# Attention scores as three reduced-precision products in a fused transformer block, with the filling jobs reordered

## The chip, the cores and the metric

The kernel runs on one NeuronCore of one Trainium2 chip. The metric is the device time of one execution in microseconds (us); several executions are timed and their median is compared. Engines: PE is TensorE (matmuls, with PEld its weight loads), DVE is VectorE, ACT is ScalarE, POOL is GpSimd, SP is SyncE, which issues most transfers.

## The reference

Four sequences of 512 tokens, width 512, 16 heads of 32, all in fp32: causal attention with residual and layer norm, then a gated feed-forward block of width 2048 with residual and layer norm.

```python
qkv = jnp.einsum('bsd,ed->bse', x, w_qkv) + b_qkv
scores = jnp.einsum('bhqd,bhkd->bhqk', q, k) / math.sqrt(Hd) + causal
attn = softmax(scores)
x = _layernorm(x + einsum(attn @ v, w_out) + b_out)
g, u = x @ Wg.T, x @ Wu.T            # weights: (integers - 128) * scale
x = _layernorm(x + (silu(g) * u) @ Wd.T)
```

## The kernel before

**Groups and steps.** The work of attention is 16 groups, G = 0 to 15: batch `b`, `g` = G % 4, four heads each (HG), whose queries or keys fill 128 partitions. Each group is run in 16 steps (STEPS) by every engine's program in the same written order: the order is fixed by hand tables, not by a scheduler, and each engine is an in-order queue.

**What a group holds.** `scores(G, qbs)` makes the scores of a 128-query tile for four heads, one product per head on its 32 rows of the array, in full fp32: `q_sb` by `k_sb`, widths 128, 256, 384, 512 by the causal mask. Tile 2 (384 wide) comes at step 0, tile 3 (512) at step 3, and tiles 0 and 1 (128 and 256) of the next group at step 8. VectorE's `tile_max` (L1131) scales, masks and takes the negative maximum; ScalarE's `exponential` (L922) follows. Ten transpose tasks (TASK_STEPS 0, 0, 3, 8, 8, 10, 10, 12, 12, 15, L1469), four 128x128 transposes each, turn the probabilities; even tasks are evicted by ScalarE (L978), odd ones by VectorE (L509). `weighted_values` (L1490) multiplies them with the values at step 8 and at the next group's step 0. `normalise`, `att_hi` and `att_lo` (L749, POOL) scale the result and split it into a high and a low fp32r part.

**Filling jobs.** Between these, TensorE works off `filling(G)`: a list of jobs of 12 products of 512 columns each (MM) and a count of products for each step. A job is the queries or the keys of the group two ahead (`project`, L1391), a value tile (`project_values`, L1409) or an output tile (`project_out`, L1427), all in three fp32r products: high by high, low by high, high by low. ENDED holds the step after that in which a job's last product stands; there the job is evicted by VectorE: `queries_or_keys` (L1117) adds the bias and writes fp32, `values` (L1122), `outputs` (L1182, with layer norm's statistics).

**Banks.** Transposes and jobs share three PSUM banks, assigned ahead by class `Banks`: the bank that was freed longest ago is next. TensorE waits (`work_drained`) until the eviction of the bank's last user is done. Four banks hold the scores, one (`pv_acc`) the weighted values.

**Other queues.** ScalarE scans the feed-forward weights for their largest value (`scan`, L942) twice in most groups, after steps 6 and 14, when a 1 MB transfer (`load_scan`) has landed; in the third group of a batch it makes the high half of the next batch's x (`next_hi`, L912, `xT_hi`), after POOL's `join`, which waits until the batch's last keys are done; POOL makes the low half (`next_lo`). SP issues transposing transfers (`turn`, `load_short`), and for w_out `turn_w`, in place of `w_stage`'s value tiles.

**Start.** Weight tiles are transposed on TensorE and split by `w_hi` (ACT) and `w_lo` (DVE) in the order of `transpose_weights`; `project` of the first batch waits for its tile's low half.

Of the kernel before, what the change touches and what calls it, by code (L numbers as in the profile page):

```python
# [6 lines left out]
def postln_block_kernel(nc: bass.Bass, x, w_qkv, b_qkv, w_out, b_out, gate_w, gate_scale, up_w, up_scale,  # L7
# [78 lines left out]
    SLOTS = 7  # L86
    X_STEPS = [1, 2, 3, 4]
    X_FIRST = [3, 4, 5, 6]
# [27 lines left out]

    def filling(G):
        b, g = divmod(G, NG)
        ahead = [("q", G + 2), ("k", G + 2)] if G + 2 < GROUPS else []
        if G == 0:  # L120
            return [("v", 0, t) for t in range(NT)], EVEN
        if G == 1:
            return [("q", 2), ("k", 2), ("q", 3)], [8, 0, 0, 4, 0, 4, 8, 0, 3, 0, 3, 0, 3, 0, 0, 3]
        if G == 2:
            return [("k", 3)] + ahead, [8, 4, 0, 0, 0, 0, 0, 0, 6, 0, 6, 0, 6, 0, 0, 6]
        if g == 0:
            return [("v", b, QH), ("v", b, QH + 1)] + ahead, EVEN
        if g == 1:
            return [("o", b - 1, 0), ("o", b - 1, 1)] + ahead, EVEN
        if g == 3:  # L130
            return ([("v", b + 1, 0), ("v", b + 1, 1)] + ahead, EVEN) if b < LAST else ([], [0] * STEPS)
        before = [("o", b - 1, t) for t in range(QH, NT)]
        return (before + ahead, AMONG_X) if b < LAST else (before, AMONG_X[:8] + [0] * (STEPS - 8))
# [7 lines left out]
    def x_at(G, s):  # L141
        return [c for c in range(ND) if (X_STEPS if G > NG else X_FIRST)[c] == s] if G % NG == 2 else []
# [17 lines left out]

    class Banks:

        def __init__(self):
            self.uses, self.ended, self.busy, self.now = [0] * (WORK + HG), list(range(-WORK - HG, 0)), {}, 0
# [18 lines left out]
        def part(self, jobs, done, count):  # L183
            for n in range(done, done + count):
# [7 lines left out]
                ("w", 3), ("q", 1), ("w", 4), ("w", 5), ("k", 1), ("w", 6), ("w", 7))  # L192
# [78 lines left out]
    with ctx:  # L271
# [34 lines left out]
        attT_hi, attT_lo, v_tok = [None] * 2, [None] * 2, [None] * 2  # L306
        attT_hi[1] = sb("attT_hi1", [P, NG, S], F32R, att)
        attT_lo[1] = sb("attT_lo1", [P, NG, S], F32R, att)
        v_tok[1] = sb("v_tok1", [P, NT, D], F32, att)
        scan_buf = sb("scan_buf", [P, NT, D], F32, att)  # L310
        attT_hi[0] = sb("attT_hi0", [P, NG, S], F32R, att)
        attT_lo[0] = sb("attT_lo0", [P, NG, S], F32R, att)
        v_tok[0] = sb("v_tok0", [P, NT, D], F32, att)
        q_sb = [sb(f"q_sb{i}", [P, S], F32, att) for i in range(2)]
        k_sb = [sb(f"k_sb{i}", [P, S], F32, att) for i in range(2)]
# [67 lines left out]
        score, work, pv_acc = bank[0:HG], bank[HG:HG + WORK] + bank[0:HG], bank[HG + WORK]  # L383
# [1356 lines left out]
```

## Time and profile before

| what | value |
|---|---|
| median of 3 runs | 728.05 us (726.4 to 728.89) |
| the profiled execution | 730.08 us |
| its span | 728.3 us |
| PE busy | 705.8 us (97%), 4296 matmul records |
| DVE, ACT, POOL busy | 385.6, 366.3, 187.7 us |
| granted TensorE clock | 0.996 of full speed |
| attention | about the first 347 us; then feed-forward |

A record of an fp32 product appears twice in the trace (two records a product); a reduced-precision product has one. A record's duration includes its way through the array, so the next one's start tells what a product costs. In the chain of waits each step is followed back to what released it; the timeline merges equal neighbours (xN).

### The profile page before, as it was taken

How to read it: one execution, taken by the hardware profiler on the slowest of the kernel's cores; microseconds unless marked ns; L12 is line 12 of the kernel's file. 1: busy time of each engine (PE TensorE's matmuls, PEld its weight loads, DVE VectorE, ACT ScalarE, POOL GpSimd, SP SyncE). 2: the span in 40 equal slices, each digit the busy share in tenths (PEclk: the TensorE clock that was granted, in tenths of full speed). 3: DMA queues.
4: the chain of work that ended last, by engine and by line, in shares of the span. 5: the costliest groups of instructions: out<-in, count | busy, mean ns of one | idle time of the engine just before them, and what ended most of it. 6: DMA issues, size and time to landing. Idle time of an engine off the chain costs nothing.

```text
span 728.3 us, 11598 instructions
## 1 busy us (share of the span) xinstructions
PE 705.8 (97%) x4296; PEld 546.0 (75%) x4296; DVE 385.6 (53%) x999; ACT 366.3 (50%) x886; POOL 187.7 (26%) x192
## 2 busy tenths in 40 slices
PE   7999899999999999999999999999999999999994
PEld 6777577677777777676687888888888888888883
DVE  3767566666667766578452223553344533544335
ACT  3766677677676766578655654222232222322230
POOL 0000633446131661219753242220010002000004
PEclk9999999999999999999999999999999999999998
DMA  9753675526774376704788944951430013000111
GB/s 306 178 140 102 154 95 189 130 75 135 171 231 96 98 146 207 216 22 125 181 154 206 198 138 144 228 187 43 145 102 13 0 43 130 1 0 1 59 58 60
DMA packets 106246, 89.33 MB, mean 123 GB/s; under 512 B 70352, under 2 KB 80592, under 8 KB 106064
## 3 DMA queue, kind: packets, MB, share of 16 engines
q1 hardware_dynamic: 99664, 68.69, 34.5%
q0 software_dynamic: 6528, 19.93, 12.4%
q8 instruction: 33, 0.54, 0.3%
q14 instruction: 21, 0.17, 0.1%
HBM read 63.20 MB, written 23.30 MB: 119 GB/s over the span
## 4 chain that ended last, share of the span: by engine, by line
PE 81%; SPq 8%; DMA 4%; POOL 2%; DVE 2%; ACT 1%; issue 1%; POOLq 0%; DVEq 0%
PE bank L1604 15%; PE bank L1605 15%; PE bank L1391 11%; PE bank L1469 8%; PE bank L1612 7%; PE bank L1611 7%; PE bank L1452 5%; PE bank L1409 5%; PE bank L1427 4%; PE bank L1490 4%; SPq L564 2%; DMA scan_buf<-in_L_ffn_up_w_dram 2%; SPq L623 1%; SPq L620 1%; SPq L626 1%; DVE probs L1131 1%
## 5 line engine op out<-in xcount | busy, mean ns | idle before, releaser
L922 ACT ACTIVATE probs<-probs,neg_max 128x128 f32<-128x128 f32 (+3 forms) x256 | 140.4, 552 | 3.3 <-DVE neg_max L1131 3.1
L1131 DVE CUSTOM_DVE_ANT_0 probs<-bank,causal 128x128 f32<-128x128 f32 (+3 forms) x256 | 110.9, 485 | 42.0 <-PE bank L1452 42.0
L1264 DVE SCALAR_TENSOR_TENSOR hid<-bank,u_scale,silu 128x512 f32<-128x512 f32 x64 | 48.0, 751 | 160.2 <-PE bank L1605 153.6
L1604 PE MATMUL bank<-xT_hi,gateT 128*128 128x512 f32 x256 | 99.9, 390 | 1.2 <-DVE hid L1264 1.2
L1605 PE MATMUL bank<-xT_lo,gateT 128*128 128x512 f32 x256 | 99.8, 390 | 0.0
L1605 PE MATMUL bank<-xT_lo,upT 128*128 128x512 f32 x256 | 99.8, 390 | 0.0
L1604 PE MATMUL bank<-xT_hi,upT 128*128 128x512 f32 x256 | 99.7, 389 | 0.0
L1469 PEld LDWEIGHTS bank<-ident,probs 128*128 128x128 f32 x640 | 71.4, 140 | 36.9 <-issue 24.1
L1030 ACT ACTIVATE silu<-bank,g_scale 128x512 f32<-128x512 f32 x64 | 44.0, 687 | 102.2 <-PE bank L1605 102.2
L1469 PE MATMUL bank<-ident,probs 128*128 128x128 f32 x640 | 88.2, 277 | 4.3 <-DVE probsT L509 1.6
L978 ACT ACTIVATE probsT<-bank 128x512 f32<-128x512 f32 x80 | 47.6, 595 | 88.4 <-PE bank L1469 86.8
L1036 ACT ACTIVATE hid_hi<-hid 128x512 fp32r<-128x512 f32 x58 | 36.7, 632 | 107.1 <-DVE hid L1264 107.1
L1612 PE MATMUL bank<-downT,hid_lo 128*128 128x512 f32 x232 | 90.4, 390 | 0.0
L1611 PE MATMUL bank<-downT,hid_hi 128*128 128x512 f32 x232 | 90.3, 389 | 0.0
L509 DVE COPY probsT<-bank 128x512 f32<-128x512 f32 x80 | 54.9, 687 | 29.2 <-PE bank L1469 29.1
L749 POOL TENSOR_TENSOR attT_lo<-attT,attT_hi 128x512 fp32r<-128x512 f32 x16 | 20.7, 1294 | 166.7 <-ACT attT_hi L934 166.7
L1268 DVE TENSOR_TENSOR hid_lo<-hid,hid_hi 128x512 fp32r<-128x512 f32 x58 | 40.2, 693 | 40.5 <-ACT hid_hi L1036 40.5
L1604 PEld LDWEIGHTS bank<-xT_hi,gateT 128*128 128x128 f32 x256 | 48.1, 188 | 11.9 <-DVE hid L1264 2.0
L1391 PE MATMUL bank<-xT_hi,wT_hi 128*128 128x512 f32 x128 | 55.6, 443 | 0.6 <-POOL xT_lo L775 0.5
L1605 PEld LDWEIGHTS bank<-xT_lo,upT 128*128 128x128 f32 x256 | 48.1, 188 | 9.9
L1605 PEld LDWEIGHTS bank<-xT_lo,gateT 128*128 128x128 f32 x256 | 48.1, 188 | 9.9
L1604 PEld LDWEIGHTS bank<-xT_hi,upT 128*128 128x128 f32 x256 | 48.1, 188 | 9.9
(111 smaller groups left out, 1164.4 us busy)
## 6 DMA issues: line engine op xcount, KB each, us to landing
halves<-x_tok SPq DMA_DIRECT2D x7, 1024.0 KB, 7.4
x_tok<-halves SPq DMA_DIRECT2D x7, 1024.0 KB, 7.9
scan_buf<-in_L_ffn_gate_w_dram SPq DMA_DIRECT2D x4, 1024.0 KB, 8.2
scan_buf<-in_L_ffn_up_w_dram SPq DMA_DIRECT2D x4, 1024.0 KB, 7.7
scan_buf<-in_L_ffn_down_w_dram SPq DMA_DIRECT2D x4, 1024.0 KB, 5.1
w_int<-in_L_ffn_gate_w_dram POOLq DMA_DIRECT2D x16, 256.0 KB, 3.4
w_int<-in_L_ffn_up_w_dram POOLq DMA_DIRECT2D x16, 256.0 KB, 3.4
w_int<-in_L_ffn_down_w_dram POOLq DMA_DIRECT2D x16, 256.0 KB, 3.6
```

The lines of the kernel that those rows point to most:

```text
L509: copy(probsT[:, (G * BLOCKS + i) % SLOTS, :], bank_of("t", G, i)[:, :]).then_inc(drained_of("t", G, i), 1)
L922: nc.scalar.activation(probs[qb][:, j, :], probs[qb][:, j, :], ACT.Exp, bias=neg_max[:, qb, j:j + 1], scale=-1.0, accum_out=row_sum[:, qb, ...
L978: evict_task(act, G, i, lambda o, i: nc.scalar.activation(o, i, ACT.Copy))
L1030: nc.scalar.activation(silu[:, i % 2, :], bank[:, :], ACT.Silu, scale=g_scale[:, i:i + 1]).then_inc(silu_done, 1)
L1131: nc.vector.tensor_tensor_reduce(out=probs[qb][:, j, :], in0=score[j][:, first:first + w], in1=causal[:, S - w:S], scale=-SCALE, scalar=-F ...
L1264: nc.vector.scalar_tensor_tensor(out=hid[:, i % 2, :], in0=bank[:, :], scalar=u_scale[:, i:i + 1], in1=silu[:, i % 2, :], op0=ALU.mult, op ...
L1391: last = nc.tensor.matmul(acc[:, :], w[:, c, e], xT[:, c, :], start=at == 0, stop=at == MM - 1)
L1469: last = nc.tensor.transpose(acc[:, m * P:(m + 1) * P], probs[qb][:, j, kb * P:(kb + 1) * P], ident[:, :])
L1604: nc.tensor.matmul(acc[n][:, :], w[:, c, cols], form(xT_hi[:, c, :]), start=c == 0, stop=False)
L1605: last = nc.tensor.matmul(acc[n][:, :], w[:, c, cols], form(xT_lo[:, c, :]), start=False, stop=c == ND - 1)
L1611: nc.tensor.matmul(down_acc[t][:, :], form(hi[:, tok]), w_down[:, i, :], start=i == 0, stop=False)
L1612: return nc.tensor.matmul(down_acc[t][:, :], form(lo[:, tok]), w_down[:, i, :], start=False, stop=i == NI - 1)
```

## The change

Scores become three fp32r products: the queries and keys are stored as a high part (`q_hi`, `k_hi`) and the rest (`q_lo`, `k_lo`). The high part is written from the bank by a new ScalarE instruction with the bias, `queries_or_keys_hi`; VectorE's then writes bank + bias - high, in place of bank + bias. The filling jobs are put in another order, so that between a group's queries and keys there is a value or output tile; the keys of G3 move from G2 to G1, with other counts. In G2 the conversions of the next x stand at steps 1 to 4 instead of 3 to 6. The attention tiles are kept in a ring of six groups in place of two sets of four. w_out's transposing transfers get a place of their own (`w_turn`). At the start the second queries go ahead of the first scores, in an eighth, spare bank (that of `pv_acc`). The variance of layer norm moves from step 9 to 11 where there are keys and queries to come.

```diff
     def filling(G):
         b, g = divmod(G, NG)
-        ahead = [("q", G + 2), ("k", G + 2)] if G + 2 < GROUPS else []
+        q, k = ([("q", G + 2)], [("k", G + 2)]) if G + 2 < GROUPS else ([], [])
...
         if G == 1:
-            return [("q", 2), ("k", 2), ("q", 3)], [8, 0, 0, 4, 0, 4, 8, 0, 3, 0, 3, 0, 3, 0, 0, 3]
+            return [("q", 2), ("k", 2), ("q", 3), ("k", 3)], [8, 0, 0, 8, 0, 8, 4, 0, 14, 0, 2, 0, 2, 0, 0, 2]
         if G == 2:
-            return [("k", 3)] + ahead, [8, 4, 0, 0, 0, 0, 0, 0, 6, 0, 6, 0, 6, 0, 0, 6]
+            return q + k, [0, 0, 0, 0, 0, 2, 4, 0, 12, 0, 2, 0, 2, 0, 0, 2]
         if g == 0:
-            return [("v", b, QH), ("v", b, QH + 1)] + ahead, EVEN
+            return [("v", b, QH)] + q + [("v", b, QH + 1)] + k, EVEN
         if g == 1:
-            return [("o", b - 1, 0), ("o", b - 1, 1)] + ahead, EVEN
+            return [("o", b - 1, 0)] + q + [("o", b - 1, 1)] + k, EVEN
...
     banks.whole(("x", 0, 0), ("w", 0), ("x", 0, 1), ("x", 0, 2), ("x", 0, 3), ("w", 1), ("q", 0), ("k", 0), ("w", 2),
-                ("w", 3), ("q", 1), ("w", 4), ("w", 5), ("k", 1), ("w", 6), ("w", 7))
+                ("w", 3))
+    banks.start(("q", 1), [SPARE_BANK])
+    banks.end(("q", 1))
+    banks.whole(("w", 4), ("w", 5), ("k", 1), ("w", 6), ("w", 7))
...
+            def queries_or_keys_hi(kind, G):
+
+                wait_full(act, kind, G)
+                if G == 0:
+                    act.wait_ge(bias_qk_loaded, 16)
+                chunk = "qk".index(kind) * NG + G % NG
+                nc.scalar.activation((q_hi, k_hi)["qk".index(kind)][G % 2][:, :], bank_of(kind, G)[:, :], ACT.Identity,
+                                     bias=bias_qk[:, chunk:chunk + 1]).then_inc(qk_hi_done, 1)
...
             for G in range(GROUPS):
                 b, g = divmod(G, NG)
                 for s in range(STEPS):
+                    for job in ENDED.get(G * STEPS + s, []):
+                        if job[0] in "qk":
+                            queries_or_keys_hi(*job)
...
             def queries_or_keys(kind, G):
 
-                wait_full(dve, kind, G)
+                dve.wait_ge(qk_hi_done, 2 * G + "qk".index(kind) + 1)
                 chunk = "qk".index(kind) * NG + G % NG
-                nc.vector.tensor_scalar((q_sb, k_sb)["qk".index(kind)][G % 2][:, :], bank_of(kind, G)[:, :],
-                                        bias_qk[:, chunk:chunk + 1], None, ALU.add).then_inc(drained_of(kind, G), 1)
+                hi, lo = ((q_hi, q_lo), (k_hi, k_lo))["qk".index(kind)]
+                nc.vector.scalar_tensor_tensor(out=lo[G % 2][:, :], in0=bank_of(kind, G)[:, :],
+                                               scalar=bias_qk[:, chunk:chunk + 1], in1=hi[G % 2][:, :].bitcast(F32),
+                                               op0=ALU.add, op1=ALU.subtract).then_inc(drained_of(kind, G), 1)
...
-                    if g == 2 and s == 9 and b > 0:
+                    if g == 2 and s == (11 if b < LAST else 9) and b > 0:
...
-                    for j in range(HG):
-                        rows = slice(j * HD, (j + 1) * HD)
-                        last = nc.tensor.matmul(score[j][:, first:first + w], q_sb[G % 2][rows, qb * P:(qb + 1) * P],
-                                                k_sb[G % 2][rows, 0:w], start=True, stop=True)
-                        if qb == qbs[-1]:
-                            last.then_inc(score_full[j], 1)
+                    for n, (qs, ks) in enumerate(((q_hi, k_hi), (q_lo, k_hi), (q_hi, k_lo))):
+                        for j in range(HG):
+                            rows = slice(j * HD, (j + 1) * HD)
+                            last = nc.tensor.matmul(score[j][:, first:first + w], qs[G % 2][rows, qb * P:(qb + 1) * P],
+                                                    ks[G % 2][rows, 0:w], start=n == 0, stop=n == 2)
+                            if qb == qbs[-1] and n == 2:
+                                last.then_inc(score_full[j], 1)
...
+            queries = project("q", 1)
+            for _ in range(MM // 2):
+                next(queries)
             scores(0, (0, 1))
-            for n, kind in enumerate("qk"):
-                for _ in project(kind, 1):
-                    pass
-                transpose_weights(2 * n + 4)
-                transpose_weights(2 * n + 5)
+            for _ in queries:
+                pass
```

**How the order moves.** ScalarE in G5 around step 7; `scan_buf` is the scan, `probsT` an evicted transpose task, `probs` an exponential. Before, and then after:

```order
L922 ACTIVATE probs,row_sum<-probs,neg_max 128x512 [waits max_done] x4
L942 ACTIVATE scan_buf,scan_sums<-scan_buf,minus_exact 128x1024 [waits scan_loaded]
L978 ACTIVATE probsT<-bank 128x512 [waits work_full0]
L922 ACTIVATE probs,row_sum<-probs,neg_max 128x128 [waits max_done] x4
L978 ACTIVATE probsT<-bank 128x512 [waits work_full0]
```
```order
L940 ACTIVATE probs,row_sum<-probs,neg_max 128x512 [waits max_done] x4
L968 ACTIVATE scan_buf,scan_sums<-scan_buf,minus_exact 128x1024 [waits scan_loaded]
L959 ACTIVATE q_hi<-bank,bias_qk 128x512 [waits work_full0]
L1012 ACTIVATE probsT<-bank 128x512 [waits work_full2]
L940 ACTIVATE probs,row_sum<-probs,neg_max 128x128 [waits max_done] x4
L1012 ACTIVATE probsT<-bank 128x512 [waits work_full2]
```

The high half of the queries stands behind the scan and ahead of task 4's eviction.

VectorE in G4 at the same steps (`v_tok` a value tile, the ISA rows 128 wide the maxima of the next group, COPY the eviction of task 3). Before, and then after:

```order
L1122 TENSOR_TENSOR v_tok<-bank,bias_v 128x512 [waits work_full0]
L1131 ISA probs,neg_max<-bank,causal 128x128 [waits score_full0]
L1131 ISA neg_max 128x1
L1131 ISA probs,neg_max<-bank,causal 128x128 [waits score_full1]
L1131 ISA neg_max 128x1
L1131 ISA probs,neg_max<-bank,causal 128x128 [waits score_full2]
L1131 ISA neg_max 128x1
L1131 ISA probs,neg_max<-bank,causal 128x128 [waits score_full3]
L1131 ISA neg_max 128x1
L509 COPY probsT<-bank 128x512 [waits work_full1]
```
```order
L1152 SCALAR_TENSOR_TENSOR q_lo<-bank,bias_qk,q_hi 128x512 [waits qk_hi_done]
L1167 ISA probs,neg_max<-bank,causal 128x128 [waits score_full0]
L1167 ISA neg_max 128x1
L1167 ISA probs,neg_max<-bank,causal 128x128 [waits score_full1]
L1167 ISA neg_max 128x1
L1167 ISA probs,neg_max<-bank,causal 128x128 [waits score_full2]
L1167 ISA neg_max 128x1
L1167 ISA probs,neg_max<-bank,causal 128x128 [waits score_full3]
L1167 ISA neg_max 128x1
L531 COPY probsT<-bank 128x512 [waits work_full0]
```

Where the second value tile was taken, the low half of the queries is, and it waits for ScalarE's.

TensorE at the start, from the fourth weight tile (`w_stage`) on. Before, and then after:

```order
L1357 MATMUL bank<-ident,w_stage 128x128 [waits work_drained0,w_loaded3]
L1357 MATMUL bank<-ident,w_stage 128x128 x3
L1452 MATMUL bank<-k_sb,q_sb 128x128 [waits work_drained1,work_drained0]
L1452 MATMUL bank<-k_sb,q_sb 128x128 x3
L1452 MATMUL bank<-k_sb,q_sb 128x256 x4
L1391 MATMUL bank<-xT_hi,wT_hi 128x512 [waits work_drained1,work_drained2]
L1391 MATMUL bank<-xT_hi,wT_lo 128x512
```
```order
L1393 MATMUL bank<-ident,w_stage 128x128 [waits work_drained0,w_loaded3]
L1393 MATMUL bank<-ident,w_stage 128x128 x3
L1427 MATMUL bank<-xT_hi,wT_hi 128x512 [waits work_drained2]
L1427 MATMUL bank<-xT_hi,wT_lo 128x512
L1427 MATMUL bank<-xT_lo,wT_hi 128x512
L1427 MATMUL bank<-xT_hi,wT_hi 128x512
L1427 MATMUL bank<-xT_hi,wT_lo 128x512
L1427 MATMUL bank<-xT_lo,wT_hi 128x512
L1489 MATMUL bank<-k_hi,q_hi 128x128 [waits work_drained1,work_drained0]
L1489 MATMUL bank<-k_hi,q_hi 128x128 x3
L1489 MATMUL bank<-k_hi,q_lo 128x128 x4
L1489 MATMUL bank<-k_lo,q_hi 128x128 x4
```

Half of the second queries' product now stands ahead of the first scores, and with it the wait for the third weight tile's low half.

## Rows read from the trace of the kernel before

**Rows 1.** Busy time by stretch, G1, G2, G3, G12: length, then each engine's busy us
```profile
47.44:67.64 20.20, 19.59 (x168) 13.87 (x172) 14.49 (x46) 13.17 (x40) 1.99 (x2) 1.00 0.44 96
...
67.64:90.10 22.46, 19.66 (x160) 13.13 (x164) 13.41 (x45) 14.39 (x42) 11.12 (x10) 1.00 0.63 158
...
90.10:111.46 21.36, 21.36 (x172) 15.44 (x176) 13.83 (x45) 14.58 (x42) 6.31 (x6) 1.00 0.74 101
...
283.95:306.84 22.89, 21.58 (x173) 15.42 (x169) 13.82 (x45) 14.46 (x42) 6.92 (x6) 1.00 0.76 233
```

**Rows 2.** Chain of waits in G3 and G14: start us, us, what (x records)
```profile
95.47 1.07 PE bank L1452 x8
...
103.47 1.40 PE bank L1391 x6
...
104.87 0.87 PE bank L1469 x8
...
328.28 0.86 PE bank L1452 x8
```

**Rows 3.** Timeline of TensorE in G3: start us, us, engine, line, operation
```profile
91.68 0.93 PE L1452 MATMUL bank<-k_sb,q_sb 32*128 32x384 f32 x8
...
101.51 0.94 PE L1452 MATMUL bank<-k_sb,q_sb 32*128 32x128 f32 x16
...
102.38 1.09 PE L1469 MATMUL bank<-ident,probs 128*128 128x128 f32 x8
...
104.70 1.04 PE L1469 MATMUL bank<-ident,probs 128*128 128x128 f32 x8
...
106.96 1.04 PE L1469 MATMUL bank<-ident,probs 128*128 128x128 f32 x8
```

**Rows 4.** Timeline of ScalarE and VectorE in G3
```profile
100.16 0.71 ACT L922 ACTIVATE probs<-probs,neg_max 128x512 f32<-128x512 f32 x1
...
100.86 1.14 ACT L942 ACTIVATE scan_buf<-scan_buf,minus_exact 128x1024 f32<-128x1024 uint32 x1
...
102.47 0.29 DVE L1131 CUSTOM_DVE_ANT_0 probs<-bank,causal 128x128 f32<-128x128 f32 x1 [0.94 <-PE bank L1452]
...
103.31 0.69 DVE L509 COPY probsT<-bank 128x512 f32<-128x512 f32 x1
...
105.72 0.69 DVE L509 COPY probsT<-bank 128x512 f32<-128x512 f32 x1
```

**Rows 5.** Groups of instructions by line and shape: busy us, mean ns, idle before
```profile
L1264 DVE SCALAR_TENSOR_TENSOR hid<-bank,u_scale,silu 128x512 f32<-128x512 f32 x64 | 48.0, 751 | 160.2 <-PE bank L1605 153.6 <-ACT silu L1030 6.6
...
L978 ACT ACTIVATE probsT<-bank 128x512 f32<-128x512 f32 x80 | 47.6, 595 | 88.4 <-PE bank L1469 86.8
```

**Rows 6.** Timeline at the start: keys' eviction, third tile, scores, second queries
```profile
17.00 0.75 DVE L1117 TENSOR_SCALAR k_sb<-bank,bias_qk 128x512 f32<-128x512 f32 x1 [1.90 <-PE bank L1391]
...
18.06 1.29 DVE L1103 TENSOR_TENSOR wT_lo<-bank,wT_hi 128x512 fp32r<-128x512 f32 x2 [0.31 <-ACT wT_hi L898]
...
18.81 0.51 PE L1391 MATMUL bank<-xT_hi,wT_hi 128*128 128x512 f32 x1
...
21.71 1.04 PE L1357 MATMUL bank<-ident,w_stage 128*128 128x128 f32 x8
```

**Rows 7.** Timeline of ScalarE: first scan of G4, G6, G8, G12
```profile
122.89 1.13 ACT L942 ACTIVATE scan_buf<-scan_buf,minus_exact 128x1024 f32<-128x1024 uint32 x1
...
166.10 1.14 ACT L942 ACTIVATE scan_buf<-scan_buf,minus_exact 128x1024 f32<-128x1024 uint32 x1
...
209.00 1.15 ACT L942 ACTIVATE scan_buf<-scan_buf,minus_exact 128x1024 f32<-128x1024 uint32 x1 [1.24 <-DMA scan_buf<-in_L_ffn_gate_w_dram]
...
297.11 1.15 ACT L942 ACTIVATE scan_buf<-scan_buf,minus_exact 128x1024 f32<-128x1024 uint32 x1 [3.88 <-DMA scan_buf<-in_L_ffn_up_w_dram]
```

**Rows 8.** Timeline of TensorE in G2: the wait before transpose task 4
```profile
80.38 0.66 PE L1469 MATMUL bank<-ident,probs 128*128 128x128 f32 x4 [1.17 <-ACT probs L922]
```

**Rows 9.** Chain of waits where the feed-forward part begins
```profile
382.99 3.97 DMA stage<-down_short
```

More of the change, by code:

```diff
@@ L141, in x_at @@
     def x_at(G, s):
-        return [c for c in range(ND) if (X_STEPS if G > NG else X_FIRST)[c] == s] if G % NG == 2 else []
+        return [c for c in range(ND) if X_STEPS[c] == s] if G % NG == 2 else []
     FILLING = [filling(G) for G in range(GROUPS)]
@@ L159, in postln_block_kernel @@
     OUT_STEP, EARLY, LATE = 2, (QH, QH + 1), (0, 1)
+    SPARE_BANK = WORK + HG
     class Banks:
         def __init__(self):
-            self.uses, self.ended, self.busy, self.now = [0] * (WORK + HG), list(range(-WORK - HG, 0)), {}, 0
+            self.uses, self.ended, self.busy, self.now = [0] * (SPARE_BANK + 1), list(range(-SPARE_BANK - 1, 0)), {}, 0
             self.count = WORK
@@ L382, in postln_block_kernel @@
         bank = [ctx.enter_context(nc.psum_tensor(f"bank{i}", [P, 512], F32)) for i in range(8)]
-        score, work, pv_acc = bank[0:HG], bank[HG:HG + WORK] + bank[0:HG], bank[HG + WORK]
+        score, work, pv_acc = bank[0:HG], bank[HG:HG + WORK] + bank[0:HG] + bank[HG + WORK:], bank[HG + WORK]
         gate_acc, up_acc, down_acc = bank[0:4:2], bank[1:4:2], bank[4:8]
@@ L408, in postln_block_kernel @@
         res_ready = sem("res_ready")
-        work_full = [sem(f"work_full{i}") for i in range(WORK + HG)]
-        work_drained = [sem(f"work_drained{i}") for i in range(WORK + HG)]
+        work_full = [sem(f"work_full{i}") for i in range(SPARE_BANK + 1)]
+        work_drained = [sem(f"work_drained{i}") for i in range(SPARE_BANK + 1)]
         x_hi_done = sem("x_hi_done")
+        qk_hi_done = sem("qk_hi_done")
         score_full = [sem(f"score_full{j}") for j in range(HG)]
@@ L574, in turn_w @@
             def turn_w():
-                for t in range(NT):
-                    wait_full(sp, "w", w_tile("v", t))
                 for e in range(2 * ND):
@@ L949, in _ @@
             x_hi(3)
-            for i in range(1, 4):
-                w_hi(i)
+            w_hi(1)
+            queries_or_keys_hi("q", 0)
+            queries_or_keys_hi("k", 0)
+            w_hi(2)
+            w_hi(3)
             for j in range(HG):
                 exponential(0, 0, j)
+            queries_or_keys_hi("q", 1)
             w_hi(4)
@@ L1426, in project_out @@
                     for n, (a, w) in enumerate(((att_hi, wT_hi), (att_hi, wT_lo), (att_lo, wT_hi))):
-                        last = nc.tensor.matmul(acc[:, :], a[:, c, tok], w[:, c, NE:NE + D], start=c == 0 and n == 0,
+                        last = nc.tensor.matmul(acc[:, :], a[:, tok], w[:, c, NE:NE + D], start=c == 0 and n == 0,
                                                 stop=c == NG - 1 and n == 2)
@@ L1478, in weighted_values @@
                     pe.wait_ge(normed, G)
+                if m == 0 and G == 0:
+                    wait_drained(pe, "q", 1)
                 hf, kb, _, qbs = TASKS[PRODUCTS[m][0]]
@@ L1516, in _ @@
             transpose_weights(3)
+            queries = project("q", 1)
+            for _ in range(MM // 2):
+                next(queries)
             scores(0, (0, 1))
[L1518 to L1522 removed]
+            for _ in queries:
+                pass
+            transpose_weights(4)
+            transpose_weights(5)
+            for _ in project("k", 1):
+                pass
+            transpose_weights(6)
+            transpose_weights(7)
             outs = [project_out(B - 1, t) for t in range(NT)]
```

47 lines of the change are left out of this document (28 added, 19 removed).

## The prediction, made before the changed kernel was run

> **What bounds it now.** I read four views, in this order: the page, the busy time by stretch, TensorE's timeline of one group, and the other engines' timeline of the same stretch. G0 to G15 are the sixteen groups in the kernel's order; a group is counted here from its 384-wide scores. The page puts TensorE at nearly all of the span. G3, like most groups, lasts 21.36 us with TensorE busy for all of it, while VectorE has 13.8 and ScalarE 14.6 us of work [rows 1]: in attention what counts is TensorE's own work, plus any wait that comes to stand in it. G1 and G2 are the exceptions, 20.20 and 22.46 us with 0.6 and 2.8 us of idle TensorE [rows 1] (the stretches there begin 1.6 us sooner, with the values' products); they have 36 projection products each instead of 48.
>
> **Scores, removed and added.** Per group and tile the full-precision score costs, up to the next work: 0.86 us (384 wide), 1.07 (512) [rows 2] and 0.87 (128 and 256 together, 101.51 to 102.38 [rows 3]), 2.80 in all. Eight records of 512 columns in 1.07 us can only be four heads side by side. 512 less 384 columns is 0.21 us more, that is 1.64 ns a column or four passes of 0.41 ns; 1280 columns make 2.10 to 2.15 us, and 0.65 to 0.70 us is switching, which stays. The change makes three passes of the same columns, with weights loaded anew for each. Two bounds for a pass: 0.41 ns a column, as above, gives 1.60 us for all and a gain of 0.53; or no pass is shorter than one 128-column load with its product, which the eight probability transposes show as 0.87/8 = 0.109 us, and a wide one costs what the reduced-precision projection costs, 1.40/6 = 0.233 us for 512 [rows 2]: 128 and 256 then take 3 x 0.11 each, 384 takes 3 x 0.17, 512 takes 3 x 0.22 to 0.233, 1.8 to 1.95 in all and a gain of 0.2 to 0.35. I take 0.33, since the loads are in the kernel: **-5.3 us** over 16 groups (-3 to -8.5).
>
> **Evicting queries and keys.** VectorE's tensor_scalar took 0.75 us from the bank [rows 6] and its successor is a scalar_tensor_tensor, 751 ns in the feed-forward part [rows 5]: nothing. New is ScalarE's copy of the high half, 0.60 us like its evictions of transposes [rows 5], 32 times. ScalarE has 14.6 busy of 21.4 us, so its sum is no bound. Its place in the queue is. In the new order the queries end with the 24th product, at step 7, where before the second value or output tile ended. On ScalarE their copy stands behind the first scan of the group; on VectorE the low half stands before the four 128-wide maxima and the eviction of transpose task 3. Task 5 and the second value tile reuse banks that these free. In G3, times from its start at 91.68: the scan starts at 9.18 and takes 1.14 [rows 4]; then high half 0.60, hand-over 0.05, low half 0.75, maxima 0.84 (102.47 to 103.31), copy of task 3 0.69, hand-over 0.05. Task 3's bank is free at scan start + 4.12, less 0.28 since the 384 and 512 scores came sooner. TensorE wants it at 13.02 (104.70 [rows 3]) less the 0.34 that the three scores save. The wait is scan start - 8.84. Before, the maxima started at 10.79 and the bank was free a microsecond before it was wanted.
> Scan starts in G3, G5, G7, G9, G11, G13 are 9.18 (one pattern; G3's row stands for six): 0.34 each, 2.0 us. G4 9.85 (122.89 [rows 7]): 1.0. G6 and G10, where ScalarE also converts the next batch's x, 10.35 (166.10): 1.5 each, 3.0. G8 10.52, late because its data came late (209.00): 1.7. G12 13.16 (297.11), data 3.9 us late: 4.3, of which the kernel already pays 1.5 (that group lasts 22.89 where others last 21.36 [rows 1]): 2.8. That is 10.5 us. VectorE then has as much left before task 5's copy as before, 2.41 us from one copy's start to the next's (103.31 to 105.72 [rows 4]), where TensorE needs 2.26 (104.70 to 106.96): 0.15 more in 11 groups, 1.65. Together **+12.2 us** (5 to 15). What is queued behind: ScalarE's exponentials 128 wide, which wait for the maxima and have slack until the group's end. The keys' copy comes at the group's end, with 3.2 us of other TensorE work (values product, 384 scores, two transpose tasks) before its bank is wanted and 1.35 of eviction: nothing, and if the second scan is late, 0.3.
>
> **G1 and G2.** The fourth keys move to G1: 12 products more there, 2.8 us, less the 0.6 it waited: +2.2. In G2 they go, and the join of the next x can start at G1's end. But nothing now stands between its 384 and 512 scores. G2 becomes 15.8 us of work (21.36 less 24 products of 0.233) and waits: 1.25 for the four maxima, 0.75 for the pieces of x, 0.95 for task 2's eviction, 0.7 for the exponentials, as ScalarE does four conversions and an extra copy there. 19.45 against 22.46 is -3.0, with +2.2: **-0.8 us** net (+0.5 to -2.5; today's G2 waits 1.17 us for the exponentials at the same task [rows 8]).
>
> **Start.** The keys' bank is full at 17.00 [rows 6]. Now ScalarE makes the high half before the third weight tile's, VectorE the low half (to 18.40) before that tile's (to 19.05), and the second queries' product, which needs the tile, goes ahead of the scores: it starts at 19.1 with TensorE idle from 17.7. Six products 1.45, scores 0.91 (17.90 to 18.81), six more 1.45: 22.9 where today it is 21.71 [rows 6]. The same chain once more (keys of group 1, two weight tiles, values wait for the last of them) adds 0.4 in G0: **+1.6 us** (0.5 to 2.5).
>
> **The rest.** The feed-forward part starts behind SyncE's row of transposing loads that begins with G14's join and ends with a load that lands at 386.96 [rows 9]; what G14 and G15 save is waited for there: **+0.6**. The ring of six for the attention tiles, the extra bank and w_turn need no new wait that comes late: the output tiles of a batch are done at the end of its successor's third group, the first of these slots is rewritten in the fourth. The variance moved to step 11 follows its last output tile, and its readers are the next group's. 128 more instructions' issue lies beside running products.
>
> **Sum**: -5.3 +12.2 -0.8 +1.6 +0.6 = +8.3 us. The profiled execution took 730.08 us (span 728.3), 2.0 above the median 728.05 of the runs; against the median: **736.4 us**. About 0.3%, 2.2 us, is what a measurement of this kernel can tell from none.
>
> **Rivals.** (a) *The hand-over hides.* The largest term hangs on a queue place that I shift by sums. Were ScalarE at the queries' copy 1 us sooner than reckoned, only G6, G8, G10 and G12 would wait, 3.5 us in all: 736.4 - 8.7 = 727.7. With 2 us, only G12, 0.8: 725.0; with 1 us and passes at column rate 724.5. The sign turns at waits of 12.2 - 8.3 = 3.9 us. For it: today's steady groups show no TensorE wait at all, and both engines are a third idle. Against it: the last exponential and the scan follow each other without a gap (100.16, 100.86 [rows 4]). (b) *It comes out even*: passes at column rate (-8.5), waits of 9 us, the rest as above: +1.9 us, 730.0. (c) *The heads don't run side by side* in reduced precision, so twelve passes stand in a row: 1280 columns x 12 x 0.41 ns = 6.3 us in place of 2.1 a group, +67 us, 803. Against it: nothing in the rows but the lack of such a product; the four heads of full precision start within one record. (d) *More waits than reckoned*, by the late data of G8 and G12 growing: waits 18 us, 742.2. That the edit leaves the scores as they were is excluded: TensorE's order has the 12 products.
>
> **Chances.** My forecast 0.48, (d) 0.12, (b) 0.13, (a) 0.25, (c) 0.02. Faster by over 0.3%: 0.25, within: 0.13, slower: 0.62. The forecast's own range is 731 to 741.5; with (a), (b) and (d), and the bounds of scores and waits, 722.5 to 744.
>
> **What would show it.** Score tiles: 512 to the next work about 0.9 us, 384 about 0.74, 128 and 256 about 0.85; 0.75, 0.70 and 0.70 would mean column rate. In G3 and G5 TensorE idle 0.3 to 0.5 us before the second value tile or task 5, released by VectorE's low half of q or its copy; in G6 and G10 1.5 to 1.8; in G12 over 4. G2 about 19, G1 about 22. If ScalarE's q copies come before 10.0 us of a group and TensorE's groups last 21.0, (a) is right and I am wrong.

## The result, and the profile after

The changed kernel took 737.72 us (median of 4 runs, 737.05 to 739.69) beside 727.22 us (725.83 to 728.89) for the kernel before in the same comparison: ratio 1.0117, interval 1.0074 to 1.0159. Slower, as predicted, and 1.3 us from the 736.4. The difference that was forecast is 8.3 us; between these medians it is 10.5, and in a later comparison (735.55 us beside 729.13, ratio 1.008, 1.0055 to 1.0105) it is 6.4. The profiled spans are 735.4 and 728.3 us, 7.1 apart. Of the experiments' executions, one of 1164.12 us among the twelve of pool_queries and one of 736.35 us, the profiled one, among the ten of both are left out of the ratios below as slow, but not out of the medians.

The page of the changed kernel, first the span, then TensorE's busy time (x instructions):

```profile
span 735.4 us, 12142 instructions
...
PE 704.1 (96%) x4552; PEld 551.8 (75%) x4552; DVE 386.2 (53%) x999; ACT 386.7 (53%) x918; POOL 188.2 (26%) x192
```

TensorE is busy 1.7 us less than before in a span 7.1 us longer: the loss is idle TensorE. Busy time by stretch for G1, G2, G3, G4, G6 and G12 (length; then PE, PEld, DVE, ACT, POOL; clock, DMA), as in [rows 1]:

```profile
48.97:72.32 23.35, 22.33 (x196) 16.62 (x192) 15.36 (x47) 15.82 (x44) 3.42 (x4) 1.00 0.39 97
72.32:92.40 20.08, 16.52 (x165) 11.24 (x162) 12.61 (x43) 15.44 (x44) 9.82 (x9) 1.00 0.44 122
92.40:113.67 21.27, 21.26 (x188) 15.86 (x184) 13.73 (x45) 15.86 (x44) 6.32 (x6) 1.00 0.88 152
113.67:135.65 21.98, 21.31 (x190) 15.87 (x186) 13.73 (x45) 17.82 (x48) 11.94 (x10) 1.00 0.52 151
157.11:180.53 23.42, 21.80 (x188) 15.75 (x185) 15.56 (x50) 17.71 (x48) 13.93 (x12) 1.00 0.35 86
289.97:312.70 22.73, 21.29 (x189) 15.87 (x185) 13.73 (x45) 15.96 (x44) 6.93 (x6) 1.00 0.77 225
```

G3 is hardly shorter (21.27 for 21.36), G4 is 0.6 us longer, G6 2.1. The scores themselves did what the sum said. The chain of waits in G3: scores 384 wide, 512 wide, 128 and 256 wide:

```profile
92.47 0.73 PE bank L1489 x12
...
96.07 0.90 PE bank L1489 x10
...
102.00 0.89 PE bank L1489 x21
```

0.73 + 0.90 + 0.89 = 2.52 us where it was 2.80 [rows 2, 3]: 0.28 saved. Behind them the first wait shows in TensorE's timeline of G3:

```profile
102.81 1.09 PE L1506 MATMUL bank<-ident,probs 128*128 128x128 f32 x8
103.92 0.50 PE L1445 MATMUL bank<-wT_hi,xT_hi 128*128 128x512 f32 x1
```

From these transposes (tasks 3 and 4) to the next work it is 1.11 us, where the trace of before has 0.85 (102.38 to 103.23). In G4, G6 and G12 waits are plain to see. TensorE's timeline of these (the bracket is the idle time before, and what ended it; L1445 is a value product, L1427 a projection):

```profile
125.87 0.50 PE L1445 MATMUL bank<-wT_hi,xT_hi 128*128 128x512 f32 x1 [0.67 <-DVE q_lo L1152]
...
165.75 0.50 PE L1427 MATMUL bank<-xT_hi,wT_hi 128*128 128x512 f32 x1 [1.19 <-POOL xT_lo L793]
...
166.99 0.50 PE L1427 MATMUL bank<-xT_hi,wT_hi 128*128 128x512 f32 x1 [0.28 <-POOL xT_lo L793]
...
302.94 0.50 PE L1445 MATMUL bank<-wT_hi,xT_hi 128*128 128x512 f32 x1 [1.45 <-DVE q_lo L1152]
```

G4 and G12 stop for the low half of the queries, as forecast. G6 stops for something that my sum did not have: the next batch's x. ScalarE and VectorE in G4, the hand-over itself:

```profile
123.23 1.13 ACT L968 ACTIVATE scan_buf<-scan_buf,minus_exact 128x1024 f32<-128x1024 uint32 x1
...
124.36 0.67 ACT L959 ACTIVATE q_hi<-bank,bias_qk 128x512 fp32r<-128x512 f32 x1
...
125.06 0.75 DVE L1152 SCALAR_TENSOR_TENSOR q_lo<-bank,bias_qk,q_hi 128x512 fp32r<-128x512 f32 x1 [3.36 <-ACT q_hi L959]
```

And GpSimd in G6, which begins at 157.11: the join, then the low halves, of which the last two end at 166.9, 9.8 us into the group. In the old order the queries' products, which read them, began at step 8, 11.5 us into the group (167.29 less 155.75 in the trace of before); now they begin at step 5, 5.9 us into it.

```profile
155.67 4.46 POOL L788 COPY x_whole<-x_tok 128x1024 uint16<-128x1024 uint16 x4 [13.24 <-PE bank L1427]
160.09 2.65 POOL L793 TENSOR_TENSOR xT_lo<-x_whole,xT_hi 128x512 fp32r<-128x512 f32 x2
...
164.42 2.52 POOL L793 TENSOR_TENSOR xT_lo<-x_whole,xT_hi 128x512 fp32r<-128x512 f32 x2
```

Where the feed-forward part begins, the chain waits 4.70 us for the landing that took 3.97 in [rows 9], and TensorE's stop behind it is 2.64 us, where the trace of before has 1.19:

```profile
389.38 4.70 DMA stage<-down_short
...
394.10 1.33 ACT downT L1034 x2
```

### The profile page after: what moved, and what is told of

It reads as the page before. It is cut to its first block, busy times and chain, and to the rows that moved or that the text cites. A ratio compares the mean times of both kernels' runs of the same rounds, so it can differ in the third digit from the quotient of the medians.

```text
span 735.4 us, 12142 instructions
## 1 busy us (share of the span) xinstructions
PE 704.1 (96%) x4552; PEld 551.8 (75%) x4552; DVE 386.2 (53%) x999; ACT 386.7 (53%) x918; POOL 188.2 (26%) x192
## 4 chain that ended last, share of the span: by engine, by line
PE 77%; ACT 6%; SPq 5%; DMA 4%; DVE 4%; POOL 2%; issue 1%; POOLq 0%; DVEq 0%
PE bank L1649 15%; PE bank L1650 15%; PE bank L1506 8%; PE bank L1427 8%; PE bank L1657 7%; PE bank L1656 7%; PE bank L1445 5%; PE bank L1529 4%; PE bank L1489 4%; PE bank L1463 4%; ACT probs L940 3%; DMA scan_buf<-in_L_ffn_up_w_dram 2%; DMA scan_buf<-in_L_ffn_gate_w_dram 2%; SPq L639 2%; SPq L642 1%; SPq L645 1%
## 5 line engine op out<-in xcount | busy, mean ns | idle before, releaser
L1506 PEld LDWEIGHTS bank<-ident,probs 128*128 128x128 f32 x640 | 69.5, 140 | 28.2 <-DVE probsT L531 12.2
L1649 PEld LDWEIGHTS bank<-xT_hi,gateT 128*128 128x128 f32 x256 | 48.1, 188 | 13.3 <-DVE hid L1300 3.4
L1427 PE MATMUL bank<-xT_hi,wT_hi 128*128 128x512 f32 x128 | 52.9, 421 | 4.7 <-POOL xT_lo L793 3.2
L768 POOL TENSOR_TENSOR attT_lo_front<-attT,attT_hi_front 128x512 fp32r<-128x512 f32 x12 | 15.5, 1291 | 137.4 <-ACT attT_hi_front L951 137.4
```

The costliest lines, as they stand in the source:

```text
L1427: last = nc.tensor.matmul(acc[:, :], w[:, c, e], xT[:, c, :], start=at == 0, stop=at == MM - 1)
L1506: last = nc.tensor.transpose(acc[:, m * P:(m + 1) * P], probs[qb][:, j, kb * P:(kb + 1) * P], ident[:, :])
L1649: nc.tensor.matmul(acc[n][:, :], w[:, c, cols], form(xT_hi[:, c, :]), start=c == 0, stop=False)
```

## The experiments

One table first, since the runs are read by the lengths of groups (us, between the starts of the 384-wide scores in each trace) and by the ratio to the kernel before. The first four experiments ran on one chip, the next seven on another, the last on a third.

| kernel | G1+G2 | G3 | G4 | G6 | G8 | G12 | median us | ratio (95%) |
|---|---|---|---|---|---|---|---|---|
| before | 42.66 | 21.36 | 21.36 | 21.36 | 21.36 | 22.89 | | |
| changed | 43.43 | 21.27 | 21.98 | 23.42 | 21.97 | 22.73 | 737.72 | 1.0117 (1.0074-1.0159) |
| copy_first | 43.44 | 21.04 | 21.04 | 23.41 | 21.05 | 21.03 | 732.79 | 1.004 (1.0004-1.0076) |
| outputs_first | 43.44 | 21.28 | 21.98 | 21.80 | 22.64 | 22.44 | 735.11 | 1.0104 (1.0055-1.0152) |
| scores_alone | 45.32 | 21.81 | 21.80 | 21.81 | 21.81 | 21.83 | 736.24 | 1.0107 (1.0059-1.0156) |
| order_alone | 41.91 | 21.30 | 21.32 | 23.52 | 21.30 | 21.30 | 730.17 | 1.0017 (0.9996-1.0037) |
| both | 43.44 | 21.02 | 21.05 | 21.82 | 27.10 | 21.03 | 731.31 | 1.0017 (0.9986-1.0048) |
| copies_alone | 43.82 | 21.32 | 21.31 | 22.07 | 23.27 | 21.83 | 733.29 | 1.004 (1.0008-1.0072) |
| pool_queries | 42.36 | 21.07 | 21.09 | 21.09 | 24.92 | 21.09 | 730.00 | 0.9995 (0.9971-1.0018) |
| changed, again | 44.90 | 21.30 | 22.00 | 23.42 | 21.88 | 22.05 | 735.55 | 1.008 (1.0055-1.0105) |
| pool_late_scan | 42.36 | 21.10 | 21.10 | 21.07 | 21.08 | 21.07 | 727.22 | 0.9963 (0.9933-0.9993) |
| before_late_scan | 42.60 | 21.35 | 21.36 | 21.38 | 21.36 | 21.36 | 729.06 | 0.9978 (0.9948-1.0008) |
| pool_late_old_start | 42.36 | 21.08 | 21.10 | 21.11 | 21.09 | 21.09 | 726.43 | 0.9956 (0.9931-0.9982) |
| scales_by_pool | 42.39 | 21.08 | 21.10 | 21.09 | 21.07 | 21.10 | 731.58 | 1.0022 (0.9992-1.0052) |

**copy_first.** The changed kernel, the first scan one step later, so behind the queries' copy on ScalarE.

```diff
-    ... for G in SCAN_GROUPS[1:] for s in (6, 14)]
+    ... for G in SCAN_GROUPS[1:] for s in (7, 14)]
```

> The changed kernel with the first scan of a group one step later, so that on ScalarE the queries' high half stands ahead of it. Theory A (the hand-over behind the scan is what costs): groups 4 and 8 fall from 21.97 us to about 21.1, G12 from 22.73 to 21.3, the plain ones from 21.28 to 21.05, and G6 and G10 from 23.43 to 21.1; in all 9 to 10 us less than the changed kernel, about 728. Theory B (in G6 and G10 the queries' product waits for the next x's low half, now that it stands three steps sooner, and the copy is not to blame there): those two stay above 22.8, the others fall as in A; 5 to 6 us less, about 732. Theory C (the loss is in the first three groups and at the end): under 1.5 us less.

Measured 732.79 us, as B had it. Busy time by stretch of G4 and G6 in this run:

```profile
114.33:135.37 21.04, 21.04 (x189) 15.96 (x186) 13.73 (x45) 17.60 (x48) 11.94 (x10) 1.00 0.54 160
156.54:179.95 23.41, 21.82 (x189) 15.75 (x185) 15.65 (x50) 17.82 (x48) 13.91 (x12) 1.00 0.35 84
```

G4 has no idle TensorE left, G3 lost 0.23, G12 1.70; so these waits were the copy's place behind the scan. G6 did not move: there the copy was never what TensorE waited for. 21.04 us is what a full group takes with the new scores.

**outputs_first.** The changed kernel, with the third groups' jobs in the old order.

```diff
-        return [("o", b - 1, QH)] + q + [("o", b - 1, QH + 1)] + k, (
+        return [("o", b - 1, QH), ("o", b - 1, QH + 1)] + q + k, (
```

> The changed kernel with the old job order in the third groups alone: both output tiles, then queries, then keys. Theory A: the queries' copy no longer stands behind the scan at step 7 in G6 and G10, their whole excess of 2.1 us over a plain group goes, 4 us less. Theory B: TensorE's stops before products that read the next x's low half (1.8 us in G6, as much in G10) go, 3.6 to 4.8 us less; the stop named there in the trace is POOL's xT_lo in the changed kernel and none here. The two agree on the sum; what tells them apart is the length of G6 in the run with the copy first. Theory C: nothing to speak of.

G6 fell by 1.6 us to 21.80, less than either theory had: the stop for xT_lo is gone, but another has come, 0.69 us before the keys' first product, released by VectorE's low half of the queries; scores_alone explains it. G8 gave 0.7 us back, its scan's data having landed later. The ratio cannot be told from the changed kernel's 1.0117; it is the trace that decides here.

**order_alone.** The kernel before with the new job order, counts and variance step; scores in full precision, one eviction.

> The kernel before (full-precision scores, one VectorE eviction) with the new job order, the new counts of G1 and G2, the earlier conversions in G2 and the later variance. Theory A: no ScalarE copy, no hand-over, so G3 to G13 stay at 21.36 and G6, G10 too; only G1 and G2 change, within 1 us: ratio 1.000. Theory B: G6 and G10 are 1.8 us longer each, plus 0.8 for G1 and G2 together: +4.4 us, 1.006.

B: G6 is 23.52 us and the stop is the same, without any copy. TensorE's timeline of this run in G6:

```profile
162.03 0.50 PE L1391 MATMUL bank<-xT_hi,wT_hi 128*128 128x512 f32 x1 [1.00 <-POOL xT_lo L775]
...
163.28 0.50 PE L1391 MATMUL bank<-xT_hi,wT_hi 128*128 128x512 f32 x1 [0.28 <-POOL xT_lo L775]
```

So the late x costs 2.2 us in each of G6 and G10 (21.36 to 23.52), 4.3 in all. G1 and G2 gain 0.75 us by their new counts. The whole, 1.0017, is not the 1.006 that B expected: it cannot be told from before. In this trace G12, whose data came sooner, is 1.6 us shorter than before, and G0 begins 1.7 us sooner.

**scores_alone.** The changed kernel with the old jobs, counts, banks and start.

> The changed kernel with the jobs, the counts, the banks and the start of the kernel before: the three-product scores and the two-part evictions alone. If the scores save what the changed kernel's groups show (0.28 us) and the copies hide, 16 groups give 4.5 us less than before, ratio 0.994, groups of 21.07 us. If the copies still stop TensorE in each group (0.25), ratio 0.999. If the old order with keys at once behind queries makes the copies stand in each other's way (what the reordering would be for), 1.005 or more.

The third case. Every group from G3 on is 21.81 us, 0.77 over the full 21.04. TensorE's timeline in G6 of this run, the keys' first product:

```profile
154.68 0.51 PE L1424 MATMUL bank<-xT_hi,wT_hi 128*128 128x512 f32 x1 [0.69 <-DVE q_lo L1149]
```

In the old order the queries end at step 10 and the keys want the bank two transpose tasks (1.0 us, 152.95 to 153.95) later, while copy and low half, one after the other, hold it for 1.5 us (153.15 to 154.62), though both engines stood idle before them. In a plain group the copy costs more here than in the new order (0.77 us against 0.27), which pays for this with the late x; in the whole time the two orders cannot be told apart (1.0107 and 1.0117).

**both.** The two edits together.

> The changed kernel with both edits: queries' high half ahead of the scan, and output tiles first in the third groups. If the two causes add up fully, G6 and G10 fall from 23.4 us to 21.1 and the time is 4.5 us below the run with the copy first alone, ratio to before 0.998. If, as the run with the scores alone suggests (21.81 us in every group), queries that end at step 10 with the keys at once behind them stop TensorE by 0.7 us, G6 and G10 come to 21.8: 3.2 us below the copy first alone, ratio 1.000.

The second case: G6 is 21.82 (the same 0.69 us stop), and the two edits give 731.31 us, no different from before. The profiled execution (736.35 us) lost 6 us in G8, where the scan's data came 14.8 us into the group.

**copies_alone.** As both, with one full-precision product a score, of the high halves:

```diff
-                    for n, (qs, ks) in enumerate(((q_hi, k_hi), (q_lo, k_hi), (q_hi, k_lo))):
...
+                        last = nc.tensor.matmul(score[j][:, first:first + w],
+                                                q_hi[G % 2][rows, qb * P:(qb + 1) * P].bitcast(F32),
+                                                k_hi[G % 2][rows, 0:w].bitcast(F32), start=True, stop=True)
```

> The same as the run with both edits, but each score is again one full-precision product, of the high halves read as fp32 (8 records in place of 12 a tile); the low halves are made and not read, so the scores leave out the low parts. What the three products save is then read directly: 0.28 us a group by the traces so far, 4.5 us in all (my prediction took 5.3; the column rate would be 8.5): this kernel should be 1.006 times the one with both edits, with groups of 21.3 us where that has 21.04.

Groups without a wait: 21.32 against 21.02, as expected; 0.28 to 0.3 us is what the scores save. The medians differ by 2.0 us, with intervals that overlap: the trace decides here, not the times.

**pool_queries.** The chain of two evictions on one bank is taken away. VectorE alone empties the bank, as before; GpSimd makes both halves later, from SBUF. The jobs of G3 on stand in the old order.

```diff
+        return G > 1 and (kind == "q" or G == 2)
...
+                if by_pool(kind, G):
+                    nc.vector.tensor_scalar(qk_full[:, :], bank_of(kind, G)[:, :],
+                                            bias_qk[:, chunk:chunk + 1], None, ALU.add).then_inc(drained_of(kind, G), 1)
...
+                nc.gpsimd.tensor_copy(hi, full).then_inc(split_hi, 1)
+                nc.gpsimd.tensor_tensor(lo, full, hi.bitcast(F32), ALU.subtract).then_inc(split_done, 1)
```

> The changed kernel with the old job order in groups 3 to 15 (first groups' new counts kept). The queries (and the keys of G2) are evicted by VectorE alone, bank plus bias in fp32, as before the change, and GpSimd makes their high and low halves from that copy later; the keys are copied as in the change. If the chain of two evictions on one bank is what costs (A), TensorE never waits in a plain group: 21.04 us, G1 and G2 together 41.4 us, about 5 to 6 us below the kernel before, ratio 0.993. Rival: GpSimd's 2.6 us a group beside VectorE's work make VectorE's instructions longer or come too late for the next scores: groups of 21.3 us or more, ratio 1.000.

A, in every group from G3 on but one. G1 and G2 together took 42.36 us where A had 41.4: there the rival is right in part, since in G1 TensorE stops 0.78 us before the next scores, released by GpSimd's low half of the keys. The ratio is 0.9995 and not the 0.993 of A. Busy time by stretch of G3, G6 and G8:

```profile
90.98:112.05 21.07, 21.07 (x188) 15.99 (x184) 13.82 (x45) 15.28 (x43) 8.22 (x8) 1.00 0.86 165
154.26:175.35 21.09, 21.09 (x188) 15.99 (x184) 15.47 (x50) 17.14 (x47) 14.71 (x12) 1.00 0.39 92
196.45:221.37 24.92, 22.70 (x189) 17.29 (x186) 13.92 (x45) 15.16 (x43) 8.68 (x8) 0.93 0.68 211
```

Neither VectorE's time (13.8 us) nor GpSimd's 2 us more cost anything. But G8 lost 3.8 us to a scan whose data came late, and ScalarE stood before it. ScalarE's timeline in G8:

```profile
210.25 1.15 ACT L994 ACTIVATE scan_buf<-scan_buf,minus_exact 128x1024 f32<-128x1024 uint32 x1 [4.82 <-DMA scan_buf<-in_L_ffn_gate_w_dram]
```

**The last comparison** has the changed kernel again, pool_queries with the first scan of G4, G8 and G12 at step 12 in place of 6, the kernel before with that alone, and the combination with the old start:

```diff
-    ... for G in SCAN_GROUPS[1:] for s in (6, 14)]
+    ... for G in SCAN_GROUPS[1:] for s in (6 if G % NG else 12, 14)]
```

> The changed kernel itself, on the same chip as the three others of this call, so that they have one reference: 1.010 to 1.013 times the kernel before. Its groups should repeat (21.28 plain, 21.97 for G4, 23.43 for G6 and G10), apart from G8 and G12, whose length goes by when the first scan's data land.

> The run with GpSimd splitting the queries, and the first scan of every batch's first group (G4, G8, G12) at step 12 in place of 6, since in its trace G8 lasted 24.92 us with the data landing 13.8 us into the group, and 27.1 in the run with both edits. If that wait is an in-order ScalarE standing before its data, G8 and G12 come to 21.1 whatever the landing, and the time to some 5 us below the kernel before: ratio 0.992. If the transfers themselves (their traffic) hold the group up, nothing changes: 0.9995.

> The kernel before with the first scans of G4, G8 and G12 at step 12 alone. In the trace of before G12 is 1.5 us longer than its neighbours and the data of G8 and G12 land late; if the later scan takes that away, 1.5 to 3 us less, ratio 0.997, and what remains between this kernel and the one with GpSimd is the scores' share, 4 us. If its groups are bound elsewhere: 1.000.

> The same as the run with the late scans and GpSimd's split, with the start of the kernel before (first scores ahead of the second queries, no spare bank). My prediction gave the new start +1.6 us over the old one without copies; with copies in both, this kernel should be 0.5 to 1 us slower if the new start helps to hide the copies, and equal within 0.3 us if the start is bound by the weight tiles alone. In the traces the time from the last x tile's first transpose to G0's 384-wide scores is to be compared (17.6 to 18.4 us with the new start, 18.1 with the old one).

The late scan does what the first case says: G8 is 21.08 us with TensorE busy throughout, although the data landed 14.8 us after their issue and 13.3 us into the group (13.6 and 13.9 in the two other kernels with GpSimd's split and the late scan), as late as in pool_queries (13.8). So it was the engine that stood before its data, and not the traffic. With it the kernel is faster than before, 727.22 and with the old start 726.43 us, ratios 0.9963 and 0.9956, 1.2% below the changed kernel on the same chip. I had expected 0.992. The kernel before gains by it too (0.9978, its interval includes 1), and G12 falls from 22.89 to 21.36. How much of the 0.4% is the three-product scores' and how much the late scan's is not shown: the intervals of 0.9956 and 0.9978 overlap. The changed kernel repeated 1.008, less than the 1.010 to 1.013 I had written. G1 and G2 were 1.5 us longer in it than in the first trace (44.90), to which the last section comes. The start can be read from the transposes of the third and fourth weight tiles, TensorE's last work before the two starts part, to G0's 384-wide scores. TensorE's timelines, of before and then of the changed kernel:

```profile
16.80 1.03 PE L1357 MATMUL bank<-ident,w_stage 128*128 128x128 f32 x8
...
26.62 0.93 PE L1452 MATMUL bank<-k_sb,q_sb 32*128 32x384 f32 x8
```
```profile
15.38 1.03 PE L1393 MATMUL bank<-ident,w_stage 128*128 128x128 f32 x8
...
26.26 0.45 PE L1489 MATMUL bank<-k_hi,q_hi 32*128 32x384 f32 x4
```

It is 9.76 to 9.82 us in the three kernels without copies, 11.18 to 11.24 with copies and the old start, 10.88 to 10.93 in the eight with copies and the new one. So the new start saves 0.3 us there, and half of it is lost in G0 (22.68 against 22.55 here): they are equal within 0.3 us, the second case of that expectation.

**scales_by_pool.** pool_late_old_start, with the three loads of the feed-forward scales issued by GpSimd instead of SyncE.

> The run with GpSimd's split, late scans and the old start, with the three loads of the feed-forward scales issued by GpSimd in place of SyncE. In the traces TensorE stops at the fifth tile of the feed-forward part for 1.58 us before the change and 2.9 to 3.3 us in every kernel with the three-product scores and GpSimd's split, and SyncE's row of transposing loads, which holds that tile's weights back, has 6.5 to 7 us of these three issues in it. If the row is what the saved time of the last groups is waited for (my term 'the rest'), the stop goes and the time falls by 3 us: ratio to the kernel before about 0.992. If the stop stays, it is released by something else.

The time did not fall: 731.58 us. The stop at the fifth tile (2.92 us in pool_late_old_start) is gone, but a new one of 7.03 us stands at the first down product, behind which TensorE comes to the fifth tile 8 us later (393.70 against 385.73), so that the missing stop tells nothing of SyncE's row. Nor did the row end sooner: its last load for that tile was issued 44.1 us after the start of G15, where pool_late_old_start has 41.7. The chain of waits of this run:

```profile
361.65 1.15 POOL u_scale L902
362.80 12.62 DMA d_scale<-in_L_ffn_down_scale_dram
```

## Why the prediction was right, and where it was not

The time and the sign were right; of the five terms that gave them the scores, the start and the counts of G1 and G2 were close, and the largest, the waits, was not. By the profiled executions (728.3 to 735.4 us):

- **Scores**, -5.3: 0.28 us a group, -4.5 over 16 (copies_alone has 0.30). The bound that I took from a load fits, though no run shows that it is the load: passes of 128 and 256 columns both follow each other by 0.11 us (102.09, 102.20, 102.31 and 102.48, 102.60 in TensorE's timeline of G3), those of 512 by 0.23. At column rate a pass of 128 columns would take 0.05; that rate, and with it the gain of 8.5 us, is not there. The Trainium skill ("TensorE: Matmul & The Clock Gate", section "Weight-path perf modes — Fast Weight Load (FWL) and DoubleRow") lets loads of 128 columns other than FP32 go faster; by that the narrow passes would be shorter, and the traces do not agree for these products on 32 rows. Mis-sized by 0.05: the narrow tiles gained nothing (0.87 to 0.89).
- **Hand-over behind the scan**, +12.2: mechanism and formula hold outside G6 and G10, its inputs did not. Measured against copy_first: about 0.27 in each of six groups, 0.94 and 0.92 in G4 and G8, 1.70 in G12, nothing in G6 and G10, 5.2 us in all; less the 1.5 that G12 paid before, 3.7 over the kernel before. "Scan start - 8.84" with the scan starts of this trace (those of G8 and G12 came 0.7 and 2.6 us sooner than in the trace of before, with 0.28 allowed for the scores) gives 0.31, 1.0, 1.0 and 1.75. I had taken the landings of one trace for fixed. The 0.15 for task 5 was wrong: where it shows (G5, G9, G13) order_alone has it without a copy.
- **G6 and G10**: I put 3.0 us on them for the copy, and they lost 4.1 over before, for another reason. I followed the queries' eviction into two queues and did not ask what their product reads. GpSimd's low halves could have been read from the trace of before; in the one after they end 166.9 - 157.1 = 9.8 us into the group.
- **G1 and G2**, -0.8: the counts gave -0.75 (order_alone). But the copies cost 2.1 us there (43.43 plus 0.56 for the scores, against 41.91), which I counted only from G3 on; in the trace TensorE stops 0.82 us in G1 and 0.84 in G2 before transposes, released by VectorE's eviction of a transposed tile (in G1 the queries' low half and four maxima stand ahead of it), and order_alone has neither stop. copy_first has the same 43.44, so it is not the scan.
- **Start**, +1.6: right. G0's scores began 0.36 us sooner than before only because this execution was 1.42 us ahead where the starts part (15.38 against 16.80, the transposes of the third and fourth weight tiles; the point lies between 14.58 and 16.80 in the traces, with either start). From there to G0 it is 10.88 us against 9.82, +1.06, and G0 lasts 0.31 longer though its scores save 0.28: +1.65 in all. The second queries' product starts 2.32 us behind that point (17.70), where I had 2.3 (19.1 less 16.80), with the 1.3 us stop before it.
- **The rest**, +0.6: +1.45, the stop of 1.19 us became 2.64. That it ends with SyncE's row the chains of waits show, before and after. But the row did not merely stay: from the start of G14 to the landing it is 59.9 us where it was 58.8, of which 0.7 is the last landing. scales_by_pool does not settle it, and in the other kernels with copies the stop is 1.45 to 2.92 us; why stays open.

So 8.5 us of the waits that I summed did not come, and 6.4 us that I had not summed did (2.1 in G1 and G2, 4.3 for the late x), with 0.8 more at each of scores and rest, 0.4 for task 5, and 1.4 less by the early beginning; 0.3 us is left open. That the forecast came within 1.3 us is luck: errors of 8.5 and 6.4 us stood against each other, and the difference itself, forecast as 8.3, was 10.5 in one comparison and 6.4 in another. Rival (a), that the hand-over hides, holds only where ScalarE's queue was cleared by hand; (b) and (c) are excluded by the passes; (d), late data, is real, but comes in some traces (G8 of pool_queries, both and copies_alone) and not in others.

## What to carry to other kernels

When a product is moved ahead in a hand-written order, look up both ends: who evicts it, and when what it reads is ready. A bank that two engines must empty one after the other is held for both and for both queues; let one engine empty it and split from SBUF on an idle one. Put a piece of work that waits for a transfer, and that nobody waits for, at the latest place in an in-order queue.

## What the hardware showed that I had not expected

A stop can cost more than its length. In G8 of pool_queries, where the scan's data came 13.8 us into the group, TensorE stood still for 2.22 us, and behind it the granted clock fell to 0.5, the lower of its two levels (1.2 GHz). Busy time by stretch there (length, PE, PEld, DVE, ACT, POOL, then the clock):

```profile
210.00:212.00 2.00, 0.00 (x0) 0.00 (x0) 0.93 (x3) 1.75 (x4) 0.00 (x0) 1.00 0.61 223
212.00:214.00 2.00, 1.98 (x9) 1.72 (x10) 0.00 (x0) 2.00 (x10) 0.00 (x0) 0.80 0.10 27
214.00:216.00 2.00, 2.00 (x10) 1.72 (x9) 1.16 (x2) 0.97 (x4) 0.44 (x1) 0.50 0.14 52
216.00:218.00 2.00, 2.00 (x10) 1.64 (x10) 0.29 (x1) 1.55 (x6) 1.46 (x2) 0.85 0.20 79
```

That group lost 3.8 us. In pool_late_old_start the stop at the fifth feed-forward tile did the same:

```profile
380.00:386.00 6.00, 3.08 (x14) 2.27 (x13) 0.75 (x1) 2.19 (x4) 1.61 (x3) 1.00 0.96 228
386.00:388.00 2.00, 2.00 (x8) 1.55 (x8) 0.69 (x1) 2.00 (x4) 0.00 (x0) 0.74 1.27 229
388.00:390.00 2.00, 2.00 (x6) 1.53 (x5) 0.00 (x0) 1.37 (x3) 0.83 (x2) 0.50 1.13 253
```

But the length of a stop does not decide it. In the changed kernel the stop of 2.64 us, which ends at 396.91, leaves the clock at 1.00, as the 1.19 us of the kernel before do:

```profile
396.00:400.00 4.00, 3.09 (x13) 2.55 (x14) 1.45 (x2) 3.11 (x7) 1.07 (x2) 1.00 0.99 179
400.00:402.00 2.00, 2.00 (x10) 1.65 (x9) 0.75 (x1) 0.85 (x2) 0.19 (x1) 1.00 1.20 243
```

And in G2 of the changed kernel's second trace the clock fell behind short stops, 0.62 and 0.76 us for ScalarE's exponentials. The first trace has the same stops at a clock of 1.00; the group took 21.57 us in place of 20.08:

```profile
80.00:82.00 2.00, 0.80 (x5) 0.57 (x6) 1.64 (x10) 1.80 (x6) 1.76 (x3) 1.00 0.00 0
82.00:84.00 2.00, 2.00 (x8) 1.71 (x8) 0.25 (x2) 0.60 (x1) 0.00 (x0) 0.52 1.43 262
```

So the same kernel pays for the clock in one execution and not in another. The stop at the fifth tile and the clock behind it are where much of the last versions' gain goes: their attention part (G0 to G15) takes 312.6 us where before has 317.5, but from the first feed-forward product to the end they take 362.9 us (725.6 - 362.7) where before has 359.8. The Trainium skill ("TensorE: Matmul & The Clock Gate", section "HAM oscillation — how this bites in real kernels") tells of products that start at the lower clock after a wait for a transfer; by that, the traces agree where a late transfer held TensorE up and the clock fell; the stop of 2.64 us, which ends behind a landing too, does not show it.

Second, one transfer's landing varies by as much as most terms of the sum: the 1 MB for G8's first scan landed 11.7, 12.8 and 15.1 us after its issue in three traces (copy_first, before, pool_queries), and that scan began 9.4 to 14.8 us into the group in the kernels that have it at step 6 or 7. Third, GpSimd's plain copy of a 128x512 tile to fp32r took 0.61 us, its subtraction 1.29 (means in pool_queries).
